# A decoder block's inner network as three f16 products of split operands

## The reference

```python
att = softmax(q k^T) v            # 16 heads of 16 channels, value bias bv
h   = relu(att @ W1 + b1)         # 256 -> 512
y   = h @ W2 + b2                 # 512 -> 256
x   = layernorm(x + y)
```

## Time and profile before

| | us |
|---|---|
| median of 3 runs | 1141.89 (1140.78 to 1142.65) |
| the profiled execution | 1142.11 |
| its span in the profile | 1140.3 |
| PE busy | 977.3 (86%) |
| PEld busy | 703.0 (62%) |
| DVE busy | 661.8 (58%) |
| ACT busy | 589.5 (52%) |
| POOL busy | 285.3 (25%) |

### The profile page before, as it was taken

The page is one execution under the profiler, slowest core; times in us unless marked ns, Lnnn a source line. Parts: engine busy times, 40 slices in busy tenths (PEclk is TensorE's granted clock), DMA queues, the critical chain, the costliest instruction groups (busy, mean ns, idle before and its releaser), DMA issues.

```text
span 1140.3 us, 22115 instructions
## 1 busy us (share of the span) xinstructions
PE 977.3 (86%) x8864; PEld 703.0 (62%) x8864; DVE 661.8 (58%) x1565; ACT 589.5 (52%) x1379; POOL 285.3 (25%) x297
## 2 busy tenths in 40 slices
PE   7987889897879898999898688888889897699995
PEld 4664556665469775567566556666666665447654
DVE  3256545665848855665666477676676664436103
ACT  5532555552548865555544355545555554465741
POOL 3421422100420007121112122122222205132733
PEclk9997878988989999999999899999899798689998
DMA  9351554300769868532261433221221105000001
GB/s 304 108 95 34 122 107 83 96 12 20 245 201 346 292 234 257 178 107 89 78 199 59 116 109 109 82 74 63 83 84 53 28 1 231 1 1 1 1 1 33
DMA packets 66678, 123.71 MB, mean 108 GB/s; under 512 B 11632, under 2 KB 41968, under 8 KB 62496
## 3 DMA queue, kind: packets, MB, share of 16 engines
q1 hardware_dynamic: 64528, 117.48, 33.8%
q0 software_dynamic: 2048, 4.82, 1.4%
HBM read 86.30 MB, written 35.92 MB: 107 GB/s over the span
## 4 chain that ended last, share of the span: by engine, by line
PE 52%; DVE 22%; ACT 10%; DMA 5%; POOL 4%; issue 4%; SPq 1%; DVEq 0%; POOLq 0%; ACTq 0%
PE psum L405 36%; ACT s_p L2738 3%; DVE s_p L2780 3%; DVE s_max L2769 2%; PE psum L1402 2%; PE psum L2708 2%; PE psum L2697 2%; DMA raw_wd<-in_wd 2%; DVE s_pT L2761 1%; POOL got L2003 1%; PE psum L2227 1%; DMA ctx_raw<-in_ctxT 1%; PE psum L560 1%; PE psum L2876 1%; DVE s_max L679 1%
## 5 line engine op out<-in xcount | busy, mean ns | idle before, releaser
L2738 ACT ACTIVATE s_p<-psum,s_max 112x375 f32<-112x375 f32 x128 | 72.2, 569 | 97.6 <-DVE s_max L2769 97.6
L726 POOL TENSOR_TENSOR rstd<-meanvar,minus_half 112x1 f32<-112x1 f32 x40 | 25.1, 629 | 244.7 <-DVE meanvar L671 174.2
L679 DVE TENSOR_REDUCE s_max<-psum 112x2 f32<-112x750 f32 x64 | 59.4, 934 | 35.7 <-PE psum L560 35.0
L2697 PE MATMUL psum<-ident,s_p 112*125 112x112 f32 x384 | 62.7, 296 | 8.9 <-DVE s_p L2780 4.2
L2769 DVE TENSOR_REDUCE s_max<-psum 112x1 f32<-112x375 f32 x128 | 63.7, 539 | 1.9 <-PE psum L2689 1.9
L2697 PEld LDWEIGHTS psum<-ident,s_p 112*125 112x125 f32 x384 | 51.3, 198 | 19.0 <-DVE s_p L2780 6.1
L3079 POOL TENSOR_TENSOR rs<-ms,minus_half 112x32 f32<-112x32 f32 x8 | 43.5, 5440 | 77.5 <-DVE ms L3013 77.5
L2689 PE MATMUL psum<-s_k,s_q 64*112 64x375 f16 x384 | 46.5, 348 | 18.5 <-ACT s_p L2738 6.3
L405 PE MATMUL psum<-Wv,ctx 128*125 128x512 f16 x240 | 58.6, 394 | 3.5 <-issue 2.7
L405 PE MATMUL psum<-ctx,Wk 128*128 128x375 f16 x320 | 61.5, 327 | 0.0
L3397 POOL TENSOR_TENSOR hidden<-raw,hidden 128x448 f16<-128x448 f32 x44 | 45.5, 1036 | 54.8 <-ACT hidden L3280 53.0
(11 more groups left out here) (381 smaller groups left out, 2465.1 us busy)
## 6 DMA issues: line engine op xcount, KB each, us to landing
keys<-s_k SPq DMA_DIRECT2D x64, 187.5 KB, 2.3
s_k<-keys SPq DMA_DIRECT2D x8, 1500.0 KB, 7.6
values<-s_v SPq DMA_DIRECT2D x48, 224.0 KB
s_v<-values SPq DMA_DIRECT2D x16, 672.0 KB
raw_wg<-in_wg SPq DMA_DIRECT2D x8, 1024.0 KB, 6.7
raw_wu<-in_wu SPq DMA_DIRECT2D x8, 1024.0 KB, 7.0
raw_wd<-in_wd SPq DMA_DIRECT2D x8, 1024.0 KB
s_kd<-k_halves SPq DMA_DIRECT2D x48, 93.8 KB, 3.8
```

Source lines behind the costliest of these rows:

```text
L679: VE.tensor_reduce(s1_max[b % 2][:, 2 * p:2 * p + 2], rings["s1"][unit][0:N, :, 0:S], X, ALU.max, negate=True).then_inc(*V.up("max1", n))
L2697: ins = TE.transpose(rings["t4"][unit][0:SCH, c * N:(c + 1) * N], p[:, c * SCH:(c + 1) * SCH], ident[0:N, 0:N])
L2738: SC.activation(rings["p4"][2 * n + j], rings["s4"][(n, j)][0:N, 0:S], ACT.Exp, bias=s4_max[b % 2][:, h:h + 1], accum_out=s4_sum[b % 2][:, ...
```

## The change

W1 and W2 are multiplied by 64 and split into an f16 high part (ACT) and an f16 low part (DVE) at the start of stage 1, in a new unit `w1s`, placed behind round 14 of the heads. W1's halves go where raw Wkv1 was. The turned attention is split too: ACT writes the high part in f16, DVE the low part from the same PSUM bank, which is free only after that. Each product of f32 becomes three of f16 (high high, high low, low high). ACT writes the hidden rows as f32 into four new buffers `s1_hf`, scaled by 1/64, and POOL makes the two f16 halves from them, with a copy and a subtraction; `out` waits for POOL. The sum of `out` is scaled by 1/64 as it is added. The planned cost of an `mlp1` unit goes from 750 to 580.

```diff
+    W1_16 = Region(nc, wts.base + split_at, 4 * KB).tensor("W1_16", [P, 2, KC, 2 * D], F16)
...
+    s1_attT = [work.tensor(f"s1_attT{i}", [P, 2, KC, 2 * N], F16) for i in range(2)]
+    s1_h = [work.tensor(f"s1_h{i}", [P, 2, 2 * KC, 2 * N], F16) for i in range(2)]
+    s1_hf = [work.tensor(f"s1_hf{i}", [P, 2 * N]) for i in range(2 * KC)]
+    W2_16 = work.tensor("W2_16", [P, 2, 2 * KC, D], F16)
...
-    step("attT1", "T attT1", "misc1", "A attT1", 150)
-    step("attT1e", "A +1, A attT1")
-    step("mlp1", "T mlp1, A mlp1", "misc1", "A mlp1", 750)
+    step("attT1", "T attT1", "misc1", "V attT1", 150)
+    step("attT1e", "A +1, A attT1, V +1, V attT1")
+    step("mlp1", "T mlp1, A mlp1, G +1, G mlp1", "misc1", "A mlp1", 580)
+    step("w1s", "A +1, A w1s, V +1, V w1s")
...
     def s1_split():
+        yield from until(("sc1", HP + 6))
+        yield [("w1s",)]
...
-                pe.wait_ge(*(A["attT1", j] for j in mlp_batches(b)), *rings["misc1"].free(unit))
+                pe.wait_ge(V["w1s",], *(V["attT1", j] for j in mlp_batches(b)), *rings["misc1"].free(unit))
                 mm(rings["misc1"][unit][:, mlp_cols(b)],
-                   [(W1[:, k, f * P:(f + 1) * P], s1_attT[b // 2 % 2][:, k, mlp_cols(b)])
-                    for k in range(KC)], T.up("mlp1", b, f))
+                   [(W1_16[:, u, k, f * P:(f + 1) * P], s1_attT[b // 2 % 2][:, v, k, mlp_cols(b)])
+                    for k in range(KC) for u, v in PARTS], T.up("mlp1", b, f))
...
-                pe.wait_ge(A["mlp1", mlp_of(b), 2 * KC - 1], *rings["misc1"].free(unit))
+                pe.wait_ge(V["w1s",], G["mlp1", mlp_of(b), 2 * KC - 1], *rings["misc1"].free(unit))
                 mm(rings["misc1"][unit][0:N, 0:D],
-                   [(s1_h[b // 2 % 2][:, k, j * N:(j + 1) * N], W2[:, k, :]) for k in range(2 * KC)],
-                   T.up("out", 1, b))
+                   [(s1_h[b // 2 % 2][:, u, k, j * N:(j + 1) * N], W2_16[:, v, k, :])
+                    for k in range(2 * KC) for u, v in PARTS], T.up("out", 1, b))
...
+            elif what == "w1s":
+                act.wait_ge(g_w1.ready)
+                SC.activation(W1_16[:, 0], W1[:], ACT.Copy, scale=WSCALE).then_inc(*A.up())
+                SC.activation(W2_16[:, 0], W2[:], ACT.Copy, scale=WSCALE).then_inc(*A.up("w1s"))
...
+            elif what == "attT1e":
+                b, = at
+                bank = rings["misc1"][("attT1", b)]
+                dve.wait_ge(A["attT1", b])
+                for c in range(KC):
+                    here = b % 2 * N
+                    VE.scalar_tensor_tensor(
+                        s1_attT[b // 2 % 2][:, 1, c, here:here + N], bank[:, c * N:(c + 1) * N],
+                        ch("bv1", c), s1_attT[b // 2 % 2][:, 0, c, here:here + N], ALU.add,
+                        ALU.subtract).then_inc(*(V.up("attT1", b) if c else V.up()))
+            elif what == "w1s":
+                dve.wait_ge(A["w1s",])
+                VE.scalar_tensor_tensor(W1_16[:, 1], W1[:], WSCALE, W1_16[:, 0], ALU.mult,
+                                        ALU.subtract).then_inc(*V.up())
+                VE.scalar_tensor_tensor(W2_16[:, 1], W2[:], WSCALE, W2_16[:, 0], ALU.mult,
+                                        ALU.subtract).then_inc(*V.up("w1s"))
             elif what == "out":
                 s, b = at
-                vector_add(1, b, 0, res, G["bias", 1, b], rings["misc1"][unit][0:N, 0:D])
+                vector_add_scaled(1, b, res, G["bias", 1, b], rings["misc1"][unit][0:N, 0:D])
...
+            elif what == "mlp1":
+                b, f = at
+                h, raw_h = s1_h[b // 2 % 2], s1_hf[f][:, mlp_cols(b)]
+                if b >= 4:
+                    pool.wait_ge(T["out", 1, max(mlp_batches(b)) - 4])
+                pool.wait_ge(A["mlp1", b, f])
+                GP.tensor_copy(h[:, 0, f, mlp_cols(b)], raw_h).then_inc(*G.up())
+                pool.wait_ge(G.so_far())
+                GP.tensor_tensor(h[:, 1, f, mlp_cols(b)], raw_h, h[:, 0, f, mlp_cols(b)],
+                                 ALU.subtract).then_inc(*G.up("mlp1", b, f))
```

More of the change, by code:

```diff
@@ L340, in build @@
     Wq1 = g_w1.load(wts, "Wq1", [P, KC, D])
+    split_at = wts.at
     Wkv1 = g_w1.load(wts, "Wkv1", [P, 2, 2 * D])
+    W1_16 = Region(nc, wts.base + split_at, 4 * KB).tensor("W1_16", [P, 2, KC, 2 * D], F16)
     Wkv1_16 = wts.tensor("Wkv1_16", [P, 4, 2 * D], F16)
@@ L1235, in build @@
     s1_att = [work.tensor(f"s1_att{i}", [N, D]) for i in range(2)]
-    s1_attT = [work.tensor(f"s1_attT{i}", [P, KC, 2 * N]) for i in range(2)]
-    s1_h = [work.tensor(f"s1_h{i}", [P, 2 * KC, 2 * N]) for i in range(2)]
+    s1_attT = [work.tensor(f"s1_attT{i}", [P, 2, KC, 2 * N], F16) for i in range(2)]
+    s1_h = [work.tensor(f"s1_h{i}", [P, 2, 2 * KC, 2 * N], F16) for i in range(2)]
+    s1_hf = [work.tensor(f"s1_hf{i}", [P, 2 * N]) for i in range(2 * KC)]
+    W2_16 = work.tensor("W2_16", [P, 2, 2 * KC, D], F16)
     s1_rs = work.tensor("s1_rs", [N, H])
@@ L1479, in scalar_s1 @@
                 for c in range(KC):
-                    SC.activation(s1_attT[b // 2 % 2][:, c, b % 2 * N:(b % 2 + 1) * N],
+                    SC.activation(s1_attT[b // 2 % 2][:, 0, c, b % 2 * N:(b % 2 + 1) * N],
                                   bank[:, c * N:(c + 1) * N], ACT.Identity,
@@ L1484, in scalar_s1 @@
                 b, f = at
-                if b >= 4:
-                    act.wait_ge(T["out", 1, max(mlp_batches(b)) - 4])
+                if b > mlp_of(0):
+                    act.wait_ge(G["mlp1", mlp_of(min(mlp_batches(b)) - 1), f])
                 act.wait_ge(T["mlp1", b, f])
-                SC.activation(s1_h[b // 2 % 2][:, f, mlp_cols(b)], rings["misc1"][unit][:, mlp_cols(b)],
-                              ACT.Relu, bias=ch("b1", f)).then_inc(*A.up("mlp1", b, f))
+                SC.activation(s1_hf[f][:, mlp_cols(b)], rings["misc1"][unit][:, mlp_cols(b)],
+                              ACT.Relu, scale=1 / WSCALE, bias=ch("b1", f)).then_inc(*A.up("mlp1", b, f))
+            elif what == "w1s":
+                act.wait_ge(g_w1.ready)
+                SC.activation(W1_16[:, 0], W1[:], ACT.Copy, scale=WSCALE).then_inc(*A.up())
+                SC.activation(W2_16[:, 0], W2[:], ACT.Copy, scale=WSCALE).then_inc(*A.up("w1s"))
             elif what == "split":
```

## The result

The changed kernel takes 1153.07 us (median of 18 executions, 1145.03 to 1159.74); the kernel before, run beside it, takes 1145.49. The ratio is 1.006 (95% interval 1.0036 to 1.0083), so the change costs 6.9 us (4.1 to 9.5). A second set of runs gave 1.0088 (1.0054 to 1.0121). The forecast was 1141.0, in a range that ended at 1147.0, and a change of -1.0 us against before. The kernel before is itself 3.6 us above the three runs that the prediction knew; even without that, the change is some 8 us worse than the -1.0 of the sum. Ratios compare executions in the undisturbed state alone, by their means (1152.21 and 1145.34 here), so they need not be the quotient of two medians.

A forecast was written before the change was run, and what follows sets the result against it. PE was taken to bound the inner network, with PE/DVE exchanges, DVE or the one-batch chain limiting elsewhere in stage 1. Terms -6.2 + 2.8 + 1.8 + 0.6 = -1.0 us gave 1141.0, range 1135.5 to 1147.0.

The forecast's parts named there:

- Part 1: `mlp1` and `out` products of pairs (0,1), (2,3), (4,5): f16 is shorter, -6.2 us, bounds 4.5 and 8.5 gained.
- Part 2: Splitting W1 and W2 behind round 14: DVE waits for ACT, PE stops; +2.8 us, bounds 0.3 and 4.5.
- Part 3: DVE's low part of the turned attention, two instructions per batch delaying maxima: +1.8 us, bounds 0.5 and 3.5.
- Part 4: POOL's halves between the layers: hidden except in the tail, batches 6 and 7; +0.6 us, bounds -1.0 and 2.5.
- `out` gains 0.5 back: Batch 7 in the tail: its shorter second-layer product returns 0.5 us against the +1.3 of waiting for POOL.
- Costed at nothing: Scaled sum, ACT's relu to other buffers, and lower planned cost moving a few norm steps under a round: no cost.
- DVE takes over: Rival, slower: around 240 to 253 DVE limits and its weight splits collide with POOL's new work; up to 1145.6; chance 0.26.
- The gain is kept: Rival, faster: the 2.53 us wait at 157.85 swallows the weight-split pause, products gain 7.2; 1137.4 us; chance 0.34.

The follow-up runs named there:

- the products alone: Changed kernel with f16 products and ACT's two weight roundings but no low parts or DVE/GpSimd additions, in the previous unit order: 1140.9 us beside 1142.96, ratio 0.9964.
- The spread version: Changed kernel with DVE's two weight low parts moved out of the pause, each alone behind a later round: 1141.77 us beside 1140.39, ratio 1.0027.
- the filled pause: Changed kernel with three unread f32 products issued by PE while it would wait for DVE's weight low parts: 1143.04 us beside 1139.69, ratio 1.0044.
- the old order: Changed kernel with the planned cost of an `mlp1` unit set back from 580 to 750, restoring the tail's previous unit order: 1147.62 us beside 1140.39, ratio 1.0078.
- GpSimd's part alone: Kernel before plus GpSimd's cast and subtraction of each hidden block, results unread, `out` waiting for them, still f32: 1145.15 us beside 1142.96, ratio 1.0032.
- the weight split alone: Kernel before plus the four weight-splitting instructions behind round 14, results unread: 1148.92 us beside 1142.96, ratio 1.0045.

## Why the prediction was wrong

**Part 1, shorter products: right.** -6.2 forecast; the products alone give -4.1 (-8.2 to +0.1), the two roundings of ACT and the gain of batches 6 and 7 included. The rows of later units gave the price: 0.75 us for a unit of `mlp1` beside 0.74.

**Part 2, the weight split: mechanism right, price too low.** The pause was read right to the detail: DVE waits for ACT's second rounding, the maximum of round 15 starts 3.25 us late (3.6 forecast), the 2.5 us wait for the queries moves along instead of swallowing it (2.26 us long in the kernel after). The step that failed is the choice of +2.8 out of 0.3 to 4.5: alone it costs +5.1 (+1.5 to +8.7), since PE, idle for 3.3 us, comes back at half clock and meets a second stretch of it from 134 to 144 us. The prediction had that only as a bound. The spread version and the filled pause are 3.8 and 5.0 us below the changed kernel, each at the edge of its uncertainty, but both lie on the expected side, and the rows go with it.

**Part 3, the low part of the turned attention: not refuted.** Two instructions a batch, together 0.56 to 0.58 us, as forecast (0.6); +1.8 forecast, +0.6 (-3.4 to +4.6) measured. What it missed is that the PSUM bank of the turn is now held until DVE is done: PE's last unit of batch 6 waits 1.61 us for the bank, of which DVE's step is the last 0.6 and ACT's the 0.6 ahead of it. With the old order the wait is 0.63 and sits ahead of work of the norm.

**Part 4, the tail: the step that failed most.** +0.6 forecast, bounds -1.0 and 2.5; the tail loses 3.0 and 3.7 us in two profiles, and GpSimd's part alone costs +3.7 (-0.6 to +7.8). Its terms were right where they were GpSimd's: 0.28 and 0.40 us for 112 columns (0.25 and 0.40 forecast), a chain of four units of 2.85 us (3.1). Batch 6 came out nearly as forecast: against the lateness at 261.8, `out` 6 starts 0.7 us later (0.4 forecast) and is shorter by 0.56 (0.5 to 1.0), 2.81 us against 3.37; in all +0.1 for -0.3. What was wrong is batch 7's other side of the sum, "`out` gains 0.5 back", and that nothing was put down for what follows it. Counted from the start of batch 7's units, `out` 7 starts 1.6 us later than before (4.68 us instead of 3.07; 1.3 forecast) and takes 0.8 more instead of 0.5 less, since it runs at half clock; what follows it, at a granted clock of 0.50 in 280 to 290 us, takes another 1.5. These 3.9 us are the tail's loss.

**Costed at nothing.** The planned cost did change the order in the tail, `out` and `mlp1` units among them, not "a few norm steps". That was a false reading of the planner, but it cost nothing that the ratios show (1.0078 with the old order; some 2 us could hide there).

**The rival "DVE takes over"** had the right sign, too low a price (+3.7 at its dearest, under the interval of 4.1 to 9.5) and, but for its bound of part 2, the wrong place. The collisions happened as the rule says that the prediction weighed (the Trainium skill, GPSIMD Engine Reference, Specifications: contention with DVE instructions of two SBUF inputs); the trace agrees, a GpSimd cast of 2.60 us instead of 0.36. But it is GpSimd that pays most (5.0 us, DVE 0.7), and GpSimd's units are covered there except for 0.27 us at `out` 4. Its chance, 0.26, was too low mostly because the clock was treated as a bound in one part and not at all in the others. **"The gain is kept"** fell with the weight split alone: the wait for the queries swallows nothing.

**The range** also fell short for a reason outside the change: it was laid around three runs of before, and before alone has medians from 1139.7 to 1145.5 in the five sets of runs. Moved up by the 3.6 us, it would end at 1150.6, still under the 1153.07.

## What to carry to other kernels

Where a change puts a wait in front of TensorE, its price is the wait and the half clock that may follow it: count what stands behind it at both levels of the clock before taking a saving on the products in that place. One-off work such as a weight split belongs in single pieces behind rounds that have room, each on an engine that needn't wait for the other; two instructions of DVE behind two of ACT cost 5 us here, and by the ratios some 4 less with DVE's two in places of their own. A step added between two layers is cheap only while another batch covers it; the last batch of this pipeline waited 1.79 and 1.95 us for it. And before a half-clock product is put down to the wait in front of it, look whether the kernel before was at half clock in that place too: here it was, at batch 6.

## What the runs showed of the hardware

- A GpSimd cast or subtraction of 128x224 beside DVE instructions of two SBUF inputs (128x1024) takes 1.36 to 2.60 and 1.47 us instead of 0.36 and 0.61; DVE's take 1.22 to 1.63 instead of 1.21. One small DVE instruction, on 112x16, took 0.75 instead of 0.17 us beside a subtraction of GpSimd's text split.
- TensorE at full clock up to an idle time of 3.29 us ran its next product at half clock. With f32 products in most of that time and a wait of 0.72 us left, it ran on at full clock and fell to half some 3 us later all the same, until about 137 us.
- In the tail, where TensorE waits 0.4 to 2 us in front of several units, a product of 1.52 us took 2.81; with one wait cut to 0.84 us by DVE it still did, with both waits filled the second one didn't. The wait right in front does not settle it: in f32, one product took 3.37 us behind 0.24 us of idle time (before) and 1.98, at full clock, behind 1.06 (GpSimd's part alone).
- On 112 columns DVE casts in 0.21 and subtracts in 0.28 us, GpSimd in 0.28 and 0.40: for so little work the two are close.
- Executions of one kernel in one set spread by more than 1% (1139.65 to 1152.75 for before, 1145.03 to 1159.74 for the changed kernel), and two profiles of one kernel show half-clock stretches at other places.
